# Second attention: ACT's copies one slot earlier, and the low parts of rotary query rows on POOL

## The reference, cut to what matters

```python
q = rmsnorm(x @ wq_a.T, q_a_ln_w) @ wq_b.T          # 16 heads of 128 + 64
q_pe, k_pe = apply_rope(q_pe), apply_rope(k_pe)      # the 64 rotary columns
q_abs = einsum('bhsd,hdc->bhsc', q_nope, q_absorb)   # 64 latent columns
scores = (q_abs @ kv.T + q_pe @ k_pe.T) * SCALE      # 128 columns in all
attn = softmax(where(causal, scores, min))
x = einsum('bhst,btc->bhsc', attn, kv)               # then out_absorb, wo
```

## Time and profile before

| | |
|---|---|
| median of 3 runs | 1639.2 us (1634.21 to 1649.61) |
| the profiled execution: its own time, its span | 1637.82 us, 1636.2 us |
| PE busy | 1300.0 us, 79% of the span |
| DVE, ACT, POOL busy | 904.1 (55%), 740.1 (45%), 501.5 us (31%) |
| granted TensorE clock, mean | 0.909 of 2.4 GHz |
| second attention, first sequence | about 768 to 1110 us |
| second attention, second sequence | about 1253 to 1592 us |

### The profile page before, as it was taken

One profiled execution on the slowest core, in us unless ns is written; L12 is line 12 of the kernel. 1 busy time (PEld: TensorE's weight loads), 2 busy tenths in 40 slices (PEclk: granted clock), 3 DMA queues, 4 the chain that ended last, 5 costly groups with the idle time before them and its releaser, 6 DMA issues. The chain is left out here.

```text
span 1636.2 us, 24271 instructions
## 1 busy us (share of the span) xinstructions
PE 1300.0 (79%) x7940; PEld 940.3 (57%) x7940; DVE 904.1 (55%) x2104; ACT 740.1 (45%) x1668; POOL 501.5 (31%) x488
## 2 busy tenths in 40 slices
PE   2666729999899839585899999997485999999977
PEld 2565615555555427474666666666474666666656
DVE  6646548777677243244666666650244666666640
ACT  1534404666565602433555555540334555555530
POOL 0222243333230000140555555520131554445520
PEclk9887959999999959787999999998797999999998
DMA  2312186555550096202100111005102001010005
GB/s 77 132 52 106 68 87 57 62 61 67 56 61 22 21 274 183 55 13 73 38 29 27 36 36 37 27 14 159 43 26 81 24 27 46 27 45 27 14 26 154
DMA packets 133170, 101.19 MB, mean 62 GB/s; under 512 B 48240, under 2 KB 120368, under 8 KB 132784
## 3 DMA queue, kind: packets, MB, share of 16 engines
q1 hardware_dynamic: 132000, 98.53, 26.8%
q10 hardware_dynamic: 1040, 1.05, 0.2%
HBM read 56.30 MB, written 34.87 MB: 56 GB/s over the span
## 5 line engine op out<-in xcount | busy, mean ns | idle before, releaser
L753 POOL TENSOR_SCALAR a_p<-a_p,a_rl 128x128 f32<-128x128 f32 (+7 forms) x256 | 215.6, 842 | 438.7 <-DVE a_rl L695 438.5
L736 ACT ACTIVATE a_p<-psum,a_nm 128x128 f32<-128x128 f32 (+7 forms) x256 | 190.2, 743 | 193.0 <-DVE a_nm L689 191.9
L1137 DVE TENSOR_REDUCE a_nmp<-psum 128x1 f32<-128x512 f32 (+3 forms) x384 | 198.9, 554 | 75.2 <-PE psum L1051 66.2
L1197 ACT ACTIVATE a_pt<-psum 128x512 f32<-128x512 f32 (+3 forms) x384 | 178.8, 490 | 130.5 <-PE psum L1066 95.5
L786 PE MATMUL psum<-ident,a_p 128*128 128x128 f32 x1152 | 187.5, 281 | 56.2 <-ACT a_pt L720 35.2
L1048 PE MATMUL psum<-a_op_k,a_op_q 128*128 128x512 f32 (+3 forms) x384 | 156.2, 417 | 40.1 <-DVE a_op_k L1186 33.0
L786 PEld LDWEIGHTS psum<-ident,a_p 128*128 128x128 f32 x1152 | 131.9, 142 | 94.4 <-ACT a_pt L720 52.1
L808 PE MATMUL psum<-a_pt,v 128*64 128x256 f32 (+1 forms) x1280 | 160.5, 373 | 2.0 <-ACT a_pt L720 2.0
L1063 PE MATMUL psum<-a_op_q,a_op_k 128*128 128x512 f32 (+3 forms) x384 | 156.9, 419 | 3.0 <-issue 2.6
L689 DVE CUSTOM_DVE_ANT_0 psum<-psum,mask_a 128x128 f32<-128x128 f32 (+3 forms) x128 | 63.7, 498 | 172.7 <-PE psum L771 172.6
L722 DVE COPY a_pt<-psum 128x512 f32<-128x512 f32 (+1 forms) x192 | 113.6, 591 | 11.9 <-PE psum L786 10.3
(11 more groups left out here) (266 smaller groups left out, 2835.0 us busy)
## 6 DMA issues: line engine op xcount, KB each, us to landing
a_swap<-a_raw SPq DMA_DIRECT2D x64, 128.0 KB, 2.3
ot_d<-a_ot SPq DMA_DIRECT2D x16, 512.0 KB, 2.6
o_ot<-ot_d SPq DMA_DIRECT2D x16, 512.0 KB, 6.4
a_raw_q<-qk_d SPq DMA_DIRECT2D x48, 128.0 KB, 5.5
a_raw_k<-qk_d SPq DMA_DIRECT2D x48, 128.0 KB, 9.4
a_wf<-wf_d SPq DMA_DIRECT2D x16, 384.0 KB, 3.4
qk_d<-p_stage_h SPq DMA_DIRECT2D x8, 512.0 KB, 2.7
qk_d<-p_stage_l SPq DMA_DIRECT2D x8, 512.0 KB, 3.4
```

What stands on the lines that cost most here:

```text
L736: e.activation(s.p[:, t % NPB, 0:(i + 1) * P], C.score[t % 2][:, 0:(i + 1) * P], ACT.Exp, scale=-1.0, bias=s.nm[:, k:k + 1], accum_out=s.l ...
L753: e.tensor_scalar(s.p[:, t % NPB, 0:(i + 1) * P], s.p[:, t % NPB, 0:(i + 1) * P], s.rl[:, k:k + 1], 1.0, ALU.mult, ALU.mult).then_inc(s.no ...
L1137: e.tensor_reduce(nmp[c][:, hd, i % 4, w:w + 1], a_banks[k % 3][:, 0:n], AX.X, ALU.max, negate=True).then_inc(a_maxed[k % 3], 1)
L1197: e.activation(pt[:, k // G0 % NPT, hd, off:HALF], b_banks[k % 3][:, off:HALF], ACT.Exp).then_inc(exped, 1)
```

## The change

`evacuate` gets another lag for ACT: with parity 1 it copies the transposes of step t - 4, which PE makes in this same slot, and no longer those of step t - 5. The copy still stands ahead of the exponential of step t in ACT's program. DVE's lag stays. The two rotary subtractions of the preparation leave DVE's slots 13 and 14 and go to POOL's slots 13 and 14 (`rest_pool`), behind POOL's division of that step; POOL waits for its own division ahead of the subtraction, and for the subtraction ahead of what follows. They count on a semaphore of their own (`qrest`), on which PE waits before step 0 of the next group, and ACT before it overwrites `raw`. Ahead of the loop the subtractions stay on DVE.

```diff
--- before.py
+++ after.py
@@ -698,7 +698,7 @@
 def evacuate(e, C, s, n, t, later, parity):
 
     core = s.core
-    tt = t - LAG - 1
+    tt = t - LAG - (1 - parity)
     if (tt < 0 and not later) or tt >= core.SI:
         return
 
@@ -1701,6 +1701,7 @@
         roped = ph.sem("roped")
         qhi = ph.sem("qhi")
         qlo = ph.sem("qlo")
+        qrest = ph.sem("qrest")
 
 
         PE_ROWS = (slice(64, 128), slice(0, 64))
@@ -1715,14 +1716,14 @@
             if k == 0:
                 e.wait_ge(wf_in[u], wf_count(g, u))
                 if later:
-                    e.wait_ge(qlo, g * 6)
+                    e.wait_ge(qlo, g * 4)
             elif not later:
                 pass
             elif k <= 2:
                 e.wait_ge(raw_out, g * 2 + k)
             else:
                 e.wait_ge(qhi, g * 6 + 2)
-                e.wait_ge(qlo, g * 6 + 2)
+                e.wait_ge(qlo, g * 4 + 2)
             c = k % 2
             m = slice(P, 2 * P) if k < 2 else slice(0, P)
             t = slice(c * HALF, (c + 1) * HALF)
@@ -1739,7 +1740,7 @@
                 e.wait_ge(lifted, g * 4 + k + 1)
                 if later and k == 0:
                     e.wait_ge(qhi, g * 6)
-                    e.wait_ge(qlo, g * 6)
+                    e.wait_ge(qrest, g * 2)
                 t = slice(k * HALF, (k + 1) * HALF)
                 e.activation(raw[:, t], place(g, k)[:, :], ACT.Copy).then_inc(raw_out, 1)
             elif k < 4:
@@ -1768,7 +1769,16 @@
                 r = PE_ROWS[hd]
                 e.wait_ge(qhi, g * 6 + 5 + hd)
                 e.tensor_tensor(q[u][hd][1][r, :], raw[r, :], q[u][hd][0][r, :].bitcast(F32),
-                                ALU.subtract).then_inc(qlo, 1)
+                                ALU.subtract).then_inc(qrest, 1)
+
+        def rest_pool(e, g, u, hd, done):
+
+            r = PE_ROWS[hd]
+            e.wait_ge(qhi, g * 6 + 5 + hd)
+            e.wait_ge(s.normed, done)
+            e.tensor_tensor(q[u][hd][1][r, :], raw[r, :], q[u][hd][0][r, :].bitcast(F32),
+                            ALU.subtract).then_inc(qrest, 1)
+            e.wait_ge(qrest, g * 2 + hd + 1)
 
         def rotate(e, g, k):
 
@@ -1786,7 +1796,8 @@
 
         AT_PE = {0: 0, 2: 1, 4: 2, 6: 3}
         AT_ACT = {0: 0, 2: 1, 4: 2, 6: 3, 12: 4, 13: 5}
-        AT_DVE = {5: 2, 7: 3, 13: 4, 14: 5}
+        AT_DVE = {5: 2, 7: 3}
+        AT_REST = {13: 0, 14: 1}
         AT_POOL = {4: 0, 5: 1, 6: 2, 7: 3, 8: 4, 9: 5}
 
         def next_pair(n, t, last, at):
@@ -1849,7 +1860,8 @@
                     if t < core.SI and t % PREP == 0:
                         g = t // PREP
                         e.wait_ge(qhi, (n * 2 + g + 1) * 6)
-                        e.wait_ge(qlo, (n * 2 + g + 1) * 6)
+                        e.wait_ge(qlo, (n * 2 + g + 1) * 4)
+                        e.wait_ge(qrest, (n * 2 + g + 1) * 2)
                     softmax_pe(e, C, s, n, t, later, score, value, KL)
                     nxt = next_pair(n, t, last, AT_PE)
                     if nxt:
@@ -1902,6 +1914,9 @@
                     if nxt:
                         g, _, k = nxt
                         rotate(e, g, k)
+                    nxt = next_pair(n, t, last, AT_REST)
+                    if nxt:
+                        rest_pool(e, *nxt, n * core.SI + t + 1)
 
                 e.wait_ge(tables, 32)
                 core.iterate(e, slot, 0)
```

## The result

The changed kernel takes 1681.9 us (median of 4 runs, 1679.6 to 1684.5), the kernel before, beside it, 1638.3 us. The ratio is 1.027, 95% interval 1.024 to 1.030: slower by 44 us. The forecast of 1673 us is 35 us above the same 1638.3. The profiled execution of the changed kernel has a span of 1682.9 us.

What follows compares the result with a forecast made beforehand. Bound: PE's bank waits for ACT's and DVE's copies in slots 12 to 19. 14 x (1.3 + 1.7) = 42, - 2.4, - 4 gives +36 us on 1637.8: 1673 us, slower by 2%, range 1660 to 1698.

Steps and rivals of the forecast that it cites:

- What bounds the kernel: Second attention: PE's transposes wait for PSUM copies by ACT and DVE; slots 12 to 19 hold about 3.5 us per group.
- Part one, the copy: ACT's copy a slot earlier: gains 0.8 us in slot 12, 0.5 in slot 13; delayed exponentials cost nothing.
- Part two, off DVE: Subtractions leave DVE at 14 boundaries: slot 14's reduction 1.3 us earlier, slot 15's 2.95 us behind it, POOL's division 1.13 us.
- Part three, the chain on POOL: Subtractions of 2.58 us queue around step 14's division; PE starts slot 16's scores 4.0 us later, net +1.3 us a boundary.
- the sum: Whole kernel: 14 x (1.3 + 1.7) = 42, - 2.4, - 4, so +36 us, 1673 us.
- Part four, the clock: Behind PE's 5.8 us wait the clock falls to 1.2 GHz for 3.3 to 6.0 us, costing 1.7 us.
- the last groups: Two groups without subtractions each win about 2 us, from slot 12 and ACT's last copy, together -4 us.
- rival 1: Behind PE's waits the clock stays at 2.4 GHz: +12 us, 1650 us; chance 0.06.
- rival 2: On POOL half the partitions cost half, 1.3 us a subtraction with waits: +6 us, 1644 us; chance 0.07.
- Rival 3: Ahead of slot 16, POOL's subtractions end in PE's shadow: 69 us faster, 1568 us; chance 0.10 with lesser forms.

## Why the prediction was right, and where it was off

**What bounds the kernel.** Right. The bank waits in slots 12 to 19 were the removable part, and they went.

**Part one, the copy.** Right in place and size: alone it measured -35 us, and 1602.6 us against the 1602 expected by the same steps. That it could be costed at nothing for the exponentials holds: ACT's wait for maxima is still 114.4 us.

**Part two, off DVE.** The spacing taken from the last group held. The timeline of DVE after:

```profile
1395.05 0.69 DVE L686 TENSOR_REDUCE a_part<-psum 128x1 f32<-128x512 f32 x1 [0.95 <-PE psum L771]
...
1397.99 0.69 DVE L686 TENSOR_REDUCE a_part<-psum 128x1 f32<-128x512 f32 x1 [0.93 <-PE psum L771]
...
1399.40 0.16 DVE L695 RECIPROCAL a_rl<-a_l 128x1 f32<-128x1 f32 x1
```

2.94 us between the reductions, against 2.95 forecast and 3.19 in the earlier trace rows. The division of step 13 takes 1.12 us, against 1.13 forecast.

**Part three, the chain on POOL.** Right, with two errors that cancel. The subtraction takes 2.34 us, not 2.58; the 2.2 us estimated from the Trainium skill (GPSIMD Engine Reference, section 3.1) are nearer, 0.14 us off against 0.24. Each is surrounded by 0.15 and 0.23 us of waits on POOL's own semaphores, where I had put 0.1 us in all. Together 2.7 us for one, as in the sum. From slot 14's reduction to slot 16's scores it was 9.2 us (1395.05 to 1404.29), as forecast (1450.6 to 1459.8), and PE's wait was 5.68, forecast 5.8. The place in the queue, behind the division whose reciprocal comes last, is shown by the version with the subtractions in slots 12 and 13. Which place matters can be read as well: the division of step 14 stands only 1.0 us behind the first subtraction (its reciprocal is there at 1399.56, it starts at 1400.54). Most of PE's wait comes from what has to follow that reciprocal, the division and then the second subtraction.

**Part four, the clock: the term that was mis-sized.** The fall came at all 14 boundaries, but it cost 2.4 us each, not 1.7 (the run with PE kept busy). 14 x 0.7 = 10 us is about the difference between 1673 and 1682. That nothing else shows in it is in part luck, since two smaller terms were off in opposite directions. With the clock up a group takes 43.2 us, 1.0 over the 42.24 before, where the sum has 1.3: 4 us too many. And the last groups gave less than the 2 us each of the sum: from POOL's first division to PE's last product with the values they take 45.9 us, against 46.7 and 46.4 before, so 0.7 each: 3 us too few. I had priced the low clock at 1.2 us for 3.4 us, from a fall in the kernel before. There part of the loss was given back at once. The timeline of PE before, in the slot 17 that follows 888.28:

```profile
892.73 1.29 PE L786 MATMUL psum<-ident,a_p 128*128 128x128 f32 x8
```

All eight transposes run through, where at 1461.26 the second four wait 0.26 us for ACT's copy. A slower PE no longer waits there, and 0.42 us (the idle time and its 0.16) of the 1.7 us comes back. In the changed kernel no such wait is left to give back, so the full half is paid.

**The last groups, and the rivals.** The clock staying up (rival 1) would have been 1649 us, by the run that keeps it up, where I had 1650. Half price for half the partitions (rival 2) is out, with 2.34 us for 64 x 1024. Rival 3 was right in that POOL's work can be put into PE's shadow, and wrong in its size: 1568 us forgot that DVE's copy in slot 16 becomes the next bound. The runs without subtractions and with early ones put it at 1591 to 1597 us.

## What to carry to other kernels

Work that goes to an idle engine is queued behind what that engine does last in the chain: read when its last input there comes into being, not how idle it is. Here 28 subtractions of 2.3 us cost 78 us in slots 13 and 14, and about 12 us of gain was to be had from moving them at all. Two slots earlier the same instructions cost nothing and the kernel is 47 us faster than before the change, 35 of them by the copy. A stall of PE of 5.7 us was paid nearly one and a half times here (2.4 us of slow work on top), since the clock fell behind it, and the price of a low clock must be read where PE has no other waits to lose.

## What the runs showed of the hardware

**The clock.** Behind 5.7 us of waiting it fell 14 times out of 14, behind 2.8 to 3.1 us 11 times out of 14. Below that the length of the wait alone does not tell: behind 2.1 us it fell 9 times out of 14 in the kernel with one subtraction on each engine, but 3 times out of 14 with both on DVE in slots 12 and 13; behind the 1.3 us of the kernel with only the copy moved never, but behind two of the 14 waits of 1.0 us in the kernel before (889.5 and 974.8). What else decides is open. Each us at 1.2 GHz past the wait cost half a us. TensorE work without use during the wait (22 matmuls of 512 columns) kept it at 2.4 GHz and won 33 us.

**POOL and DVE on SBUF.** A subtraction of two SBUF tiles on DVE and a division on POOL hold each other up, and the one that starts second pays. DVE's subtraction takes 1.20 us where it comes first and 1.87 us where POOL's division came first; POOL's division of 1024 columns takes 1.13 us alone and 1.90 us behind the start of a subtraction. The Trainium skill (SBUF — State Buffer, Who interferes with whom) says that whichever starts first keeps the shared port pair for its whole instruction, and the trace agrees to 0.13 us: 0.80 us left of the division (0.91 - 0.11) and 1.20 us of its own make 2.00, against 1.87 measured. POOL's subtraction beside DVE's reductions and copies out of PSUM kept its 2.33 to 2.40 us in every run.

**POOL on 64 partitions.** POOL's two-input instruction takes 2.34 us for 1024 elements on 64 partitions and 1.29 us for 512 on 128: both handle 65536 elements, so it is the elements per partition that count.
